# Gathering back the experts' rows: paced gathers, three pairs written back from ScalarE's loop, and slot numbers converted in an operation of their own

## The chip, the cores and the metric

The kernel runs on one core of a Trainium2 chip. The metric is the device time of one launch in microseconds. Three runs of the kernel before took 565.52, 563.89 and 565.66 us, with a median of 565.52 us. All times of the trace are counted from the start of the profiled execution's span.

## The reference, cut to what matters

The input x has 8 sequences of 256 tokens with 128 features. Four layers are applied, each as x + layer(layernorm(x)): a state-space block A with four heads, an expert block, a selective-scan block B (Mamba), and the same expert block again. The change concerns the expert block:

```python
logits = hidden @ router_w.T                  # 2048 tokens x 16 experts
top_vals, top_idx = top_k(logits, 1)          # one expert for each token
scores = sigmoid(top_vals)                    # at the chosen expert, 0 elsewhere
routed_in = hidden * score                    # only the chosen expert's row is not zero
gate, up = split(routed_in @ gate_up_proj[e])
expert_sum = (up * silu(gate)) @ down_proj[e]
shared = (silu(hidden @ Wg.T) * (hidden @ Wu.T)) @ Wd.T
return shared + expert_sum
```

## The kernel before, in words

Tokens lie on the 128 partitions in 16 blocks; four blocks are a group of 512 tokens (g = 0 to 3). Each engine has one program, written out in order, and the programs meet only at semaphores. A `Signal` is a semaphore whose value is known for each event; `wait_ge` on an engine blocks everything behind it on that engine.

**The expert block** runs twice, as turn t = 0 (after block A) and turn t = 1 (after the scan, to the end of the kernel). For each group, `choose` picks the expert of each token. `rank` on TensorE counts, and `place` on VectorE (line 977 on) turns the counts into the row of a DRAM tensor `by_expert` at which each token's features are kept, so that the tokens of one expert lie together. `place` multiplies the ranks by the one-hot choice and reduces by a maximum, written as an integer into `position` (line 983). GpSimd then sends the scaled rows with indirect DMAs (`send`, line 1794), one for each block of 128 tokens.

The rows come back as 31 slots of 128 rows, in 16 pairs: pair k holds slots 2k and 2k+1, and the last pair (k = 15) holds slot 30 alone. SyncE fetches 27 slots and ScalarE four (line 1563). For each pair TensorE computes gate and up (`expand`, line 732) and down (`contract`, line 744). ScalarE applies Silu (`gate_slots`, line 1552) and copies the product out of PSUM (`take_contracted`, line 1557), always two pairs behind. The results are then written back to `by_expert`: SyncE does it for pairs 0 to 13 (line 1943), in order, and ScalarE for pairs 14 and 15, which are `LAST_PAIRS`, in a loop of its own after the last copy (line 1577). Each of these DMAs moves one slot (64 KB) and is preceded by small register operations; the registers with the slots' addresses are loaded beforehand (line 1560 for ScalarE).

When all 31 slots are written back (`put_back`), GpSimd gathers the rows for the 16 blocks with indirect DMAs into `gathered` (line 1831). The gathers of group 2 wait for those of group 0 to land, and those of group 3 for those of group 1. VectorE adds a group to x when its four gathers have landed (`land`, line 1227; in turn 0 GpSimd does group 3, line 1870). Meanwhile TensorE works on the shared expert of groups 2 and 3 (line 680 for gate and up, line 693 for down, which VectorE adds to x at line 1167).

In turn 0 `enter_scan` follows: VectorE adds group 0 and takes its moments, ScalarE makes the root, VectorE scales, and TensorE turns the block (line 442) after its down product for group 2. In turn 1 each group of x goes to the output in one DMA of 256 KB from SyncE (line 1948) as soon as it is complete, and the kernel ends with the one of group 3.

**The scan** has 64 steps. In each step VectorE does two products (line 1290) and two scans (line 1296), GpSimd two products (line 1877) and ScalarE two exponentials (line 1685). Routing work of groups that are finished is put between the steps, among it `place` for groups 0, 1 and 2 of turn 1.

## Time and profile before

| | |
|---|---|
| median of three runs | 565.52 us |
| time of the profiled execution | 565.52 us |
| its span | 564.2 us |
| TensorE, VectorE busy | 467.7 us, 413.9 us |
| ScalarE, GpSimd busy | 317.0 us, 319.3 us |
| 32 indirect gathers (line 1831) | 31.5 us on GpSimd, 985 ns each |
| turn 0: first gather starts | 209.00 us |
| turn 1: first gather starts | 538.03 us |

The span is the time from the first to the last record of the execution; 1.3 us of the time lie outside it. A long row of busy shares says little here, because the stages have different limits: the stages have to be looked at one by one, with the chain of work that ended last.

### The profile page before, as it was taken

How to read it: one execution, taken by the hardware profiler on the slowest of the kernel's cores; microseconds unless marked ns; L12 is line 12 of the kernel's file. 1: busy time of each engine (PE TensorE's matmuls, PEld its weight loads, DVE VectorE, ACT ScalarE, POOL GpSimd, SP SyncE). 2: the span in 40 equal slices, each digit the busy share in tenths (PEclk: the TensorE clock that was granted, in tenths of full speed). 3: DMA queues.
4: the chain of work that ended last, by engine and by line, in shares of the span. 5: the costliest groups of instructions: out<-in, count | busy, mean ns of one | idle time of the engine just before them, and what ended most of it. 6: DMA issues, size and time to landing. Idle time of an engine off the chain costs nothing.

```text
span 564.2 us, 7407 instructions
## 1 busy us (share of the span) xinstructions
PE 467.7 (83%) x2102; PEld 267.8 (47%) x2102; DVE 413.9 (73%) x824; ACT 317.0 (56%) x656; POOL 319.3 (57%) x298
## 2 busy tenths in 40 slices
PE   0994878897979999989797998869776876799996
PEld 0742455565746985363232344223332331459973
DVE  4278969687256426399999799999999799564333
ACT  2574274655262644567674877787656952345611
POOL 1019743352544217246779778999799876442164
PEclk9997898998679999989998999999888989989999
DMA  8999930000004331155554455547544552014432
GB/s 292 424 327 333 322 132 1 1 2 20 19 29 120 111 113 52 51 159 138 157 150 133 130 157 149 138 130 185 153 133 127 166 150 56 20 48 118 125 82 89
DMA packets 39991, 73.94 MB, mean 131 GB/s; under 512 B 4368, under 2 KB 20240, under 8 KB 39184
## 3 DMA queue, kind: packets, MB, share of 16 engines
q1 hardware_dynamic: 35600, 67.00, 39.8%
q0 software_dynamic: 2048, 4.20, 2.5%
q10 hardware_dynamic: 2304, 2.29, 1.3%
q8 instruction: 17, 0.28, 0.2%
q14 instruction: 22, 0.18, 0.1%
HBM read 66.00 MB, written 26.28 MB: 164 GB/s over the span
## 4 chain that ended last, share of the span: by engine, by line
PE 35%; DVE 25%; issue 16%; ACT 13%; POOL 8%; DMA 2%; SPq 0%; DVEq 0%; POOLq 0%; ACTq 0%
DVE arena L1296 9%; PE psum L680 7%; PE psum L732 5%; POOL arena L1877 3%; PE psum L862 3%; DVE psum L1290 3%; ACT L1374 3%; POOL arena L1831 3%; PE psum L693 3%; PE psum L744 2%; ACT arena L1685 2%; PE psum L781 2%; ACT xn L1404 2%; PE psum L666 1%; PE psum L510 1%
## 5 line engine op out<-in xcount | busy, mean ns | idle before, releaser
L1877 POOL TENSOR_TENSOR arena<-arena 128x512 f32<-128x512 f32 x127 | 158.2, 1270 | 54.4 <-DVE arena L1296 54.1
L862 PE MATMUL psum<-arena,w 128*128 128x512 f32 x256 | 135.7, 645 | 28.2 <-POOL arena L1877 25.9
L1296 DVE TENSOR_TENSOR_SCAN arena<-arena,psum 128x512 f32<-128x512 f32 x128 | 148.4, 1200 | 7.7 <-ACT arena L1685 4.1
L1685 ACT ACTIVATE arena<-arena 128x510 f32<-128x510 f32 x128 | 87.2, 713 | 41.8 <-DVE arena L1296 39.4
L862 PEld LDWEIGHTS psum<-arena,w 128*128 128x128 f32 x256 | 45.4, 198 | 103.7 <-POOL arena L1877 79.5
L1290 DVE TENSOR_TENSOR psum<-psum,arena 128x512 f32<-128x512 f32 x128 | 81.5, 681 | 1.0 <-DMA arena<-bc_store 0.9
L680 PE MATMUL psum<-xnt,w 128*128 128x512 f32 x128 | 63.0, 643 | 0.0
L1762 POOL TENSOR_TENSOR arena<-arena 128x512 f32<-128x512 f32 x16 | 20.3, 1266 | 72.3 <-DVE arena L995 72.3
L1831 POOL DMA_INDIRECT arena<-by_expert,routes x32 | 31.5, 985 | 28.3 <-DMA by_expert<-arena 19.2
L1161 DVE TENSOR_TENSOR arena<-psum,arena 128x512 f32<-128x512 f32 x24 | 16.5, 690 | 34.0 <-PE psum L680 27.4
L1794 POOL DMA_INDIRECT by_expert<-xn,routes x32 | 32.3, 1008 | 13.7 <-issue 7.9
L680 PEld LDWEIGHTS psum<-xnt,w 128*128 128x128 f32 x128 | 25.5, 208 | 29.1 <-issue 28.6
L1374 ACT ACT_TABLE_LOAD x25 | 32.1, 1283 | 9.1 <-DMA c<-c_in 8.7
L732 PE MATMUL psum<-arena 128*128 128x128 f32 x248 | 33.1, 276 | 2.4 <-issue 2.4
L442 PE MATMUL psum<-w,xn 128*128 128x128 f32 x64 | 12.9, 347 | 26.4 <-DVE xn L945 13.2
L693 PEld LDWEIGHTS psum<-w,arena 128*128 128x128 f32 x256 | 30.5, 197 | 5.7 <-issue 5.7
L1527 ACT ACTIVATE arena<-psum 128x512 f32<-128x512 f32 x24 | 14.3, 596 | 33.4 <-PE psum L680 33.4
L1811 POOL COPY arena<-w 128x256 f32 x30 | 12.2, 414 | 36.1 <-PE psum L732 36.1
L1216 DVE TENSOR_TENSOR arena<-psum,arena 128x256 f32<-128x256 f32 (+1 forms) x32 | 13.3, 417 | 25.8 <-PE psum L744 18.4
L693 PE MATMUL psum<-w,arena 128*128 128x128 f32 x256 | 30.8, 280 | 1.8 <-DVE arena L1161 1.8
L732 PEld LDWEIGHTS psum<-arena 128*128 128x128 f32 x248 | 30.2, 192 | 2.8 <-issue 2.8
L781 PE MATMUL psum<-xnt,arena 128*128 128x512 f32 (+3 forms) x64 | 30.0, 600 | 0.0
(197 smaller groups left out, 815.5 us busy)
## 6 DMA issues: line engine op xcount, KB each, us to landing
arena<-bc_store SPq DMA_DIRECT2D x64, 512.0 KB, 4.9
by_expert<-w_in SPq DMA_DIRECT2D x4, 4096.0 KB, 43.3
w<-w_in SPq DMA_DIRECT2D x1, 4427.5 KB, 13.0
by_expert<-arena SPq DMA_DIRECT2D x56, 64.0 KB, 1.6
arena<-by_expert SPq DMA_DIRECT2D x54, 64.0 KB, 2.0
by_expert<-w_in SPq DMA_DIRECT2D x1, 1984.0 KB, 67.0
x<-x_in SPq DMA_DIRECT2D x4, 256.0 KB, 7.4
out<-x SPq DMA_DIRECT2D x4, 256.0 KB, 2.3
```

Source lines behind the costliest of these rows:

```text
L680: nc.tensor.matmul(b, weights[:, P * c:P * c + P], xnt_group(g), start=True, stop=True).then_inc(*made.inc((t, g, c)))
L693: r = nc.tensor.matmul(b[:, P * q:P * q + P], act_of(t, g)[:, c, P * q:P * q + P], wt("shared_down")[:, DM * c:DM * c + DM], start=(c == 0 ...
L732: r = nc.tensor.matmul(b[:, P * (2 * q + half):P * (2 * q + half) + P], chosen[s % len(chosen)][:, EF * half:EF * half + EF], xs_t[:, P * ...
L781: r = nc.tensor.matmul(by_sequence(b)[:, :, back:SEQ], taps[:, DC - 1 - back, P * c:P * c + P], by_sequence(xnt_group(g))[:, :, 0:SEQ - ba ...
L862: nc.tensor.matmul(bank(6 + c), ident, state[c][s % 3], start=False, stop=(n == DS - 1)).then_inc(*summed.inc((s, c)))
L1290: nc.vector.tensor_tensor(bank(2 + c), bank(c), bc_row[i][:, 0, :], ALU.mult).then_inc(*driven.inc((s, c)))
L1296: nc.vector.tensor_tensor_scan(state[c][s % 3], decay_b[c][s % 2], bank(2 + c), 0.0, ALU.mult, ALU.add).then_inc(*state_ready.inc((s, c)))
L1374: nc.scalar.preload_act_table_set(name)
L1685: nc.scalar.activation(live, seq, ACT.Exp, scale=a_neg[:, DS * c + n:DS * c + n + 1]).then_inc(*decay_ready.inc((s, c)))
L1794: nc.gpsimd.indirect_dma_start(by_expert, bass.IndirectOffsetOnAxis(position[:, j:j + 1], 0), xn[:, j, :], None).then_inc(*scatter[n // 2] ...
L1831: nc.gpsimd.indirect_dma_start(gathered[:, j, :], None, by_expert, bass.IndirectOffsetOnAxis(position[:, j:j + 1], 0)).then_inc(*read_back ...
L1877: nc.gpsimd.tensor_tensor(state[c][s % 3], state[c][s % 3], bc_row[s % len(bc_row)][:, 1, :], ALU.mult).then_inc(*y_done.inc((s, c)))
```

## The change

There are three edits. The first makes `place` write its maximum, now a sum, as a float, and adds a copy on VectorE which converts it to an integer in a tile of its own. The second makes the last three pairs ScalarE's (slots 26 to 30, five DMAs instead of three) and issues each pair's DMAs right after that pair's copy out of PSUM, inside the loop, instead of after the loop. The third changes the waits ahead of the gathers: in turn 0 each group from the second on waits until the group before it has landed, and in turn 1 group 2 waits for group 1 and there is no other wait.

```diff
-        routes = sb("routes", [P, NBLK * NE // 2 + 4 * NBLK])
+        routes = sb("routes", [P, NBLK * NE // 2 + 5 * NBLK])
...
-        LAST_PAIRS = range(n_pairs - 2, n_pairs)
+        LAST_PAIRS = range(n_pairs - 3, n_pairs)
...
-                nc.vector.tensor_reduce(position[:, js], by_token(own), AX.X, ALU.max).then_inc(*placed.inc((n, g)))
+                step(nc.vector.tensor_reduce(position[:, js], by_token(own), AX.X, ALU.add))
+                after_steps()
+                nc.vector.tensor_copy(position_int[:, js], position[:, js]).then_inc(*placed.inc((n, g)))
...
                     nc.scalar.activation(y_rows[:, s0:s0 + m, :], pair_bank[t, "down", k][:, 0:P * m].rearrange("p (q c) -> p q c", q=m),
                                          ACT.Copy).then_inc(*y_ready.inc((t, k)))
+                    if k in LAST_PAIRS:
+                        act.wait_ge(*y_ready[t, k])
+                        for s in pairs[k]:
+                            nc.scalar.dma_start(places[s], y_rows[:, s, :]).then_inc(*put_back[t].inc(s))
+
...
-                for k in LAST_PAIRS:
-                    act.wait_ge(*y_ready[t, k])
-                    for s in pairs[k]:
-                        nc.scalar.dma_start(places[s], y_rows[:, s, :]).then_inc(*put_back[t].inc(s))
                 for c in range(NSC):
                     shared(2, c)
...
                 for g in GROUPS:
-                    if g >= 2:
-                        pool.wait_ge(*read_back[g - 2][t, GB * (g - 1) - 1])
+                    if g == 2 or (g and t == 0):
+                        pool.wait_ge(*read_back[g - 1][t, GB * g - 1])
```

The indirect DMAs of lines 1794 and 1831 take their offsets from `position_int` instead of `position`.

## Rows read from the trace of the kernel before

**Rows 1.** The page: each engine's busy time, share of the span, instructions.
```profile
PE 467.7 (83%) x2102; PEld 267.8 (47%) x2102; DVE 413.9 (73%) x824; ACT 317.0 (56%) x656; POOL 319.3 (57%) x298
```
**Rows 2.** Chain that ended last, 555 us to the end: start, length, what.
```profile
557.39 3.78 DMA arena<-by_expert,routes
...
561.19 0.69 DVE x L1227
```
**Rows 3.** The same chain, 532 to 538 us.
```profile
536.15 1.61 DMA by_expert<-arena
```
**Rows 4.** Timeline of GpSimd, turn 1's gathers: start, length, engine, line, [idle before].
```profile
538.03 0.99 POOL L1831 DMA_INDIRECT arena<-by_expert,routes  x1 [9.82 <-DMA by_expert<-arena]
...
548.19 0.94 POOL L1831 DMA_INDIRECT arena<-by_expert,routes  x1 [0.30 <-issue]
...
555.69 1.39 POOL L1831 DMA_INDIRECT arena<-by_expert,routes  x1 [0.30 <-issue]
```
**Rows 5.** Line 1831, all 32 gathers: from issue to landing.
```profile
DMA to landing us min/median/max: 2.4/2.5/4.2
```
**Rows 6.** Timeline of VectorE at the end of turn 1.
```profile
555.58 1.28 DVE L1227 TENSOR_TENSOR x<-x,arena 128x512 f32<-128x512 f32 x2
559.65 0.69 DVE L1167 TENSOR_TENSOR x<-psum,x 128x512 f32<-128x512 f32 x1 [2.79 <-PE psum L693]
```
**Rows 7.** Line 1948, the outputs of groups 1 and 2, issued from 556.28 us.
```profile
DMA to landing us min/median/max: 2.3/2.9/3.5
```
**Rows 8.** Timeline of ScalarE, turn 1, the last three copies and the DMAs behind.
```profile
533.03 0.89 ACT L1557 ACTIVATE arena<-psum 128x256 f32<-128x256 f32 x2 [0.17 <-PE psum L744]
534.09 0.28 ACT L1557 ACTIVATE arena<-psum 128x128 f32<-128x128 f32 x1 [0.17 <-PE psum L744]
534.23 1.42 ACTq L1577 DMA_DIRECT2D by_expert<-arena  x3
535.75 0.60 ACT L1527 ACTIVATE arena<-psum 128x512 f32<-128x512 f32 x1 [1.38 <-PE psum L680]
```
**Rows 9.** Line 1577 in turn 1: ns least, median, most; time to landing.
```profile
L1577 ACTq DMA_DIRECT2D by_expert<-arena x3: 338/362/369, 534.2 to 535.3; - x3
...
DMA to landing us min/median/max: 1.7/1.8/1.9
```
**Rows 10.** Timeline of SyncE, 535.5 to 536 us: two of its DMAs back to back.
```profile
535.66 0.90 SPq L1943 DMA_DIRECT2D by_expert<-arena  x2
```
**Rows 11.** Timeline of VectorE: `place` in the scan, and two dependent small operations.
```profile
413.15 0.23 DVE L983 TENSOR_REDUCE routes<-psum 128x4 int32<-128x64 f32 x1
...
166.35 0.17 DVE L1186 TENSOR_REDUCE arena<-arena 128x1 f32<-128x16 f32 x1
166.56 0.15 DVE L1188 TENSOR_SCALAR arena<-arena 128x1 int32<-128x1 f32 x1
```
**Rows 12.** Timelines of GpSimd and VectorE in the scan, behind `place` of two groups.
```profile
419.19 2.50 POOL L1877 TENSOR_TENSOR arena<-arena 128x512 f32<-128x512 f32 x2 [0.23 <-DVE arena L1296]
...
375.04 2.33 DVE L1296 TENSOR_TENSOR_SCAN arena<-arena,psum 128x512 f32<-128x512 f32 x2 [1.36 <-issue]
```
**Rows 13.** Timeline of ScalarE at the start of turn 0's expert pairs.
```profile
175.01 0.60 ACT L1527 ACTIVATE arena<-psum 128x512 f32<-128x512 f32 x1 [1.12 <-PE psum L680]
177.55 1.88 ACTq L1563 DMA_DIRECT2D arena<-by_expert  x4
179.88 0.60 ACT L1542 ACTIVATE arena<-psum 128x512 f32<-128x512 f32 x1 [4.27 <-PE psum L717]
```
**Rows 14.** Timelines of ScalarE, GpSimd and VectorE, turn 0's write-back and gathers.
```profile
204.44 0.89 ACT L1557 ACTIVATE arena<-psum 128x256 f32<-128x256 f32 x2 [0.17 <-PE psum L744]
...
209.00 1.02 POOL L1831 DMA_INDIRECT arena<-by_expert,routes  x1 [9.38 <-DMA by_expert<-arena]
...
216.54 0.68 DVE L1227 TENSOR_TENSOR x<-x,arena 128x512 f32<-128x512 f32 x1
...
231.32 0.69 DVE L1161 TENSOR_TENSOR arena<-psum,arena 128x512 f32<-128x512 f32 x1 [3.38 <-PE psum L680]
```

More of the change, by code:

```diff
@@ L219, in build @@
         one_hot16 = routes[:, 0:NBLK * NE // 2].bitcast(BF16)
-        top, best, score, position = (routes[:, NBLK * NE // 2 + NBLK * i:NBLK * NE // 2 + NBLK * (i + 1)] for i in range(4))
-        position = position.bitcast(I32)
+        top, best, score, position, position_int = (routes[:, NBLK * NE // 2 + NBLK * i:NBLK * NE // 2 + NBLK * (i + 1)] for i in range(5))
+        position_int = position_int.bitcast(I32)
         piece = carve()
@@ L1793, in send @@
                 for j in js:
-                    nc.gpsimd.indirect_dma_start(by_expert, bass.IndirectOffsetOnAxis(position[:, j:j + 1], 0),
+                    nc.gpsimd.indirect_dma_start(by_expert, bass.IndirectOffsetOnAxis(position_int[:, j:j + 1], 0),
                                                  xn[:, j, :], None).then_inc(*scatter[n // 2].inc(j))
@@ L1827, in experts @@
                 for g in GROUPS:
-                    if g >= 2:
-                        pool.wait_ge(*read_back[g - 2][t, GB * (g - 1) - 1])
+                    if g == 2 or (g and t == 0):
+                        pool.wait_ge(*read_back[g - 1][t, GB * g - 1])
                     for j in blocks(g):
                         nc.gpsimd.indirect_dma_start(gathered[:, j, :], None, by_expert,
-                                                     bass.IndirectOffsetOnAxis(position[:, j:j + 1], 0)).then_inc(*read_back[g].inc((t, j)))
+                                                     bass.IndirectOffsetOnAxis(position_int[:, j:j + 1], 0)).then_inc(*read_back[g].inc((t, j)))
             for value, tile in ((1e-5, eps_ln), (1e-6, eps_rms), (float(np.pi / 2), quarter_turn), (1.0, one)):
```

## The prediction

> **What bounds the kernel now.** I read the page first: TensorE is busy for 467.7 us and VectorE for 413.9 us of 564.2 [rows 1]. No engine fills the span, so the stages must be taken singly, by the chain of work that ended last. At the end it runs through the gathers: the sixteenth starts at 557.39 us, lands 3.78 us later, at 561.17, and VectorE adds its group at 561.19 [rows 2]. Followed back, the gathers on GpSimd stand end to end from 538.03 us on, 1.25 us apart (0.94 busy, 0.30 issue) [rows 4], and the first one waits for a write-back of SyncE issued at 536.15 that takes 1.61 us, to 537.76 [rows 3]. So in turn 1 the write-back, the gathers and their landing are all on the path; a delay there is paid in full, less what the last landing gives back. In the scan VectorE's operations follow each other without idle time before them [rows 11], so a small operation added there is paid unless the engine idles later. In turn 0 the gathers feed VectorE's addition at 216.54 [rows 14] and have cover.
>
> **Part 1, the conversion.** `place` runs eight times. Each time a copy of 128x4 is added, and a wait between it and the reduction. The nearest pair is a reduction at 166.35 and the dependent small operation at 166.56: 0.21 us from start to start [rows 11]. I take 0.21 us each. The reduction itself stays at 0.23. Of the eight, the three of turn 0's groups 0 to 2 stand between other work of block A, and I cost them at nothing; the two of the groups 3 stand before the shared expert's products. If that cover were gone they would cost 5 x 0.21 = 1.05 us. In the scan there are three. Behind group 0's, VectorE idles for 1.36 us at 375.04, which ScalarE's work sets, so 0.21 is absorbed. Behind group 1's, at 413.15, GpSimd waits for VectorE at 419.19 [rows 11, 12] and passes the delay on; group 2's is like it. That is 2 x 0.21 = 0.42 us. Bounds: 0 if both are absorbed, 0.63 if all three pass.
>
> **Part 2, the write-back.** ScalarE loads two more addresses ahead of its fetches. Between its product's end at 175.61 and its first fetch at 177.55 it loads seven, 0.28 us each; two more make 0.55. Its fetches then end at 179.43 + 0.55 = 179.98, and with a gap of 0.10 (from the end of an issue at 535.65 to 535.75, [rows 8]) the first slots' copy starts at 180.08 instead of 179.88 [rows 13]: 0.20 us on TensorE's first pair. Between nothing and 0.55, I take 0.20, and nothing in turn 1.
>
> Now turn 1's last copies. Pair 13's copy starts at 533.03 and is over after half of 0.89, at 533.47. From a copy's start to the DMA behind it at 534.23 there are 0.14 for registers [rows 8]. Two DMAs of one pair are (1.42 - 0.37) / 2 = 0.53 apart and one takes 0.37 [rows 8, 9]. ScalarE waits for its own copy before it issues, so copy and issue no longer overlap, and the next copy stands behind the issues:
> pair 13: issues 533.61 and 534.14, free at 534.51; pair 14: copy 534.61 to 535.05, issues 535.19 and 535.72, free at 536.09; pair 15: copy 536.19 to 536.47, issue 536.61, landing 1.8 later [rows 9], at 538.41.
> SyncE loses two DMAs at 0.49 each (535.66 to 536.15, [rows 3, 10]) and its last lands at 537.76 - 0.98 = 536.78. So the last write moves from SyncE to ScalarE, and from 537.76 to 538.41: the gathers start 0.65 us later. The other end is 0.98 earlier, if SyncE still lands last. What ScalarE does next, the Silu at 535.75, comes some 1.3 us later, but its engine stood idle there and TensorE has a long down product before it needs that bank, so I cost it at nothing.
>
> **Part 3, the waits before the gathers.** In turn 1 group 2's first gather (548.19) now waits for the gather just before it, issued 1.25 us earlier, which lands after 2.5 us, the median [rows 4, 5]. With the 0.27 us from landing to start (537.76 to 538.03) this gather starts 2.77 us after its predecessor instead of 1.25: 1.52 us more. Queued behind it on GpSimd are seven gathers and nothing else; behind them VectorE's last addition and the output. The old waits cost nothing (0.30 us, as before every gather), and neither does dropping that of group 3. The last gather starts at 557.39 + 0.65 + 1.52 = 559.56.
> Its landing is the one place that gives back. It took 3.78 us beside two outputs of 256 KB issued from 556.28, which themselves took 2.3 and 3.5 us [rows 2, 7]. The new start is about when these end, so I take the median of 2.5 [rows 5] and get 562.06, 0.89 us later than 561.17. With 3.8 it would be 2.2 later.
> One gather, at 555.69, takes 1.39 instead of 0.94 us; it starts just after VectorE's addition at 555.58 [rows 4, 6]. I keep its 0.45. The Trainium skill (SBUF — State Buffer, on the port pair that VectorE and GpSimd share) says the pair is locked for a whole instruction when VectorE reads two SBUF inputs, and the second to come blocks. By that rule this row is a blocked gather, and since the additions of groups 1 and 2 will no longer be adjacent there may be two of them, 0.45 us more; if the starts miss each other it is 0.45 less.
> The skill's DMA: Bandwidth & Descriptors (the section on one GpSimd DMA) gives about 2.0 us fixed plus bytes over 436 GB/s, estimated 2.15 us for 64 KB. The trace has 2.5. By the page the stall would be 1.17 us and the sum 0.7 lower (stall and last landing).
>
> In turn 0 the same arithmetic on the copies from 204.44 on gives a last landing at 204.44 + 5.38 = 209.82 and the first gather at 210.09 instead of 209.00. The group's fourth starts 3.8 us later and lands at 216.4, against the addition at 216.54 [rows 14]: just hidden. Then each group waits. Group 1 starts at 216.7 and lands at 223.0, group 2 starts at 223.3 and lands at 229.6. VectorE idles for 3.38 us before 231.32 [rows 14]; the addition and moments of group 2 move into that gap. Group 3's addition waits on GpSimd, in the scan. Cost: nothing.
>
> **The sum.** 0.42 + 0.20 + 0.89 = 1.51 us on a profiled execution of 565.52 us (span 564.2 and 1.32 around it), which is also the median: 567.0 us. About 0.3% (1.7 us) is what a measurement of this kernel can tell from no change, and the sum lies just under it.
>
> **Rivals.**
> *SyncE still lands last.* ScalarE's issues are quick; the gathers start 0.98 earlier and the stall of 1.52 leaves the last at 557.93. For it: issue slots on ScalarE overlapped its copy at 534.23 [rows 8]. Against: the new wait is on the copy just made. Landing in 3.2, between the ends, at 561.1, the tail is even, and 0.62 remains: 566.1 us.
> *The gathers leave the end* (not slower). The stall is small and the last gather lands unhindered before VectorE's down addition ends at 560.34 [rows 6], so the last addition follows at 560.36 instead of 561.19: 0.83 us gained, 565.3 us, or 564.7 with the copies absorbed. It decides once the last gather lands before 560.34, so it must start by 557.8; my sum has it 1.7 us later.
> *The last landing stays at 3.8 us.* The outputs move later too, since group 2 lands later. 568.3 us.
> *Turn 0's waits show.* The place is VectorE's addition of group 0: its cover is only 0.14 us, and group 2's fills the 3.38 us almost wholly. If a gather there lands in 3.5 instead of 2.5 us, group 0 is about 1 us late, and everything up to the scan with it: 568.0 us or more.
> *The change does not do what it says* exists in a small form: in turn 0 it spaces gathers whose landing nobody awaits sooner. It is in the forecast.
>
> **How the numbers follow.** Forecast 0.55 (own range 566.0 to 568.0), SyncE last 0.13, gathers leave the end 0.10, landing stays long 0.12, turn 0 shows 0.10. The range from 564.8 to 568.9 reaches from the third case through the fourth; executions before spread down to 563.89. Slower by over 0.3% (above 567.2) holds some two fifths of the forecast and most of the last two cases: 0.43. Faster by over 0.3% needs the third case and the spread: 0.06. The rest, 0.51, is within 0.3%.
>
> **What would show it.** Part 1: a copy after each of the eight reductions, 0.2 us, and the end of the scan some 0.4 to 0.6 us later. Part 2: ScalarE's copies of pairs 14 and 15 about 1.1 us and 2.1 us later, its last issue near 536.6 (plus 0.6 from before), and the first gather released by ScalarE's DMA. Part 3: in turn 1 an idle time of 1.8 us on GpSimd before the ninth gather and no other, in turn 0 three such. Wrong would be a first gather earlier than 538.0, a last landing before 560.3, or an idle TensorE in 216 to 236 us.

## The result, and the profile after

The change makes the kernel slower. 15 runs of it have a median of 568.62 us (565.58 to 573.11), 15 runs of the kernel before, on the same chip, 565.52 us (562.94 to 567.87); the ratio is 1.0068 with a 95% interval of 1.0042 to 1.0095, so +3.8 us (+2.4 to +5.4). A ratio here is the one on record, worked out over all runs of both kernels, and not the quotient of the two medians: many runs of the kernel before lie close to 563 us or close to 567 us, and a median of a dozen jumps between the two. The forecast was 567.0 us, with "within 0.3%" as the likeliest outcome. Its sum was too small.

The profiled execution of the changed kernel spans 569.1 us against 564.2, 4.9 more. The page's first part, for [rows 1]:
```profile
PE 468.3 (82%) x2101; PEld 267.8 (47%) x2102; DVE 416.4 (73%) x832; ACT 316.7 (56%) x656; POOL 318.1 (56%) x298
```
VectorE has 8 instructions more and 2.5 us more of work. Eight copies at the forecast 0.21 us would be 1.7. Where the rest sits shows in the row of the copies' line; its columns are least, median and most ns, first and last start, shapes:
```profile
L985 DVE CAST routes<-routes x8: 169/183/1066, 116.6 to 498.2; 128x4 int32<-128x4 f32 x8
```
The median of 0.18 us is near what was forecast, and one copy takes 1.07 us. The timeline of VectorE finds it (start, length, engine, line, operation); the first three rows are group 1's `place` in the scan of turn 1, the rest is group 2's:
```profile
414.76 0.20 DVE L981 TENSOR_TENSOR psum<-psum,routes 128x64 f32<-128x64 f32 x1
415.00 0.23 DVE L983 TENSOR_REDUCE routes<-psum 128x4 f32<-128x64 f32 x1
415.26 0.24 DVE L985 CAST routes<-routes 128x4 int32<-128x4 f32 x1
...
474.96 0.20 DVE L981 TENSOR_TENSOR psum<-psum,routes 128x64 f32<-128x64 f32 x1
475.20 0.23 DVE L983 TENSOR_REDUCE routes<-psum 128x4 f32<-128x64 f32 x1
475.46 1.07 DVE L985 CAST routes<-routes 128x4 int32<-128x4 f32 x1
476.44 1.28 DVE L1292 TENSOR_TENSOR psum<-psum,arena 128x512 f32<-128x512 f32 x2
```
GpSimd's timeline at both places says why:
```profile
412.98 4.95 POOL L1880 TENSOR_TENSOR arena<-arena 128x512 f32<-128x512 f32 x4
...
474.01 2.49 POOL L1880 TENSOR_TENSOR arena<-arena 128x512 f32<-128x512 f32 x2 [0.93 <-DVE arena L1298]
476.58 0.23 POOL L1781 TENSOR_SCALAR routes<-routes 128x4 f32<-128x4 f32 x1
```
Two products of about 1.25 us start at 474.01 and 475.23. The copy starts 0.23 us into the second and is over with it, at 476.5. Group 1's copy starts at 415.26, just before the second of its four products ends (at 415.48), and is over at 415.51. A copy that meets a product lasts until the product ends; it is short or long by where in the product it starts.

To see what this does to the end, I compared the start of the same VectorE instruction in both traces, counted from the start of the span. The shift grows by 1.10 us at this copy (from 2.13 to 3.23), and is 4.71 at the additions near 541 us. The part before the scan (+1.8) is not the change's: such shifts lay between -2.2 and +3.9 in the other profiled executions, of both signs. Inside the scan 0.35 us is added ahead of this copy, 0.28 of it at group 1's; group 0's 0.28 is there at 357 us and gone by 380, as was forecast. Behind the copy another 1.5 us is added, between the router's last products and the expert pairs. This is TensorE there, before and after:
```profile
494.28 10.34 PE L680 MATMUL psum<-xnt,w 128*128 128x512 f32 x20
...
508.02 0.60 PE L717 MATMUL psum<-w,arena 128*128 128x128 f32 x4
```
```profile
497.45 9.12 PE L680 MATMUL psum<-xnt,w 128*128 128x512 f32 x20
...
511.08 0.63 PE L717 MATMUL psum<-w,arena 128*128 128x128 f32 x4 [0.93 <-DMA arena<-by_expert]
```
The twenty products of the shared expert take 1.2 us less after, and the first product of an expert now waits 0.93 us for its fetched rows. From the first of them to the expert it is 13.7 us before and 13.6 after: next to nothing gained. The cause of the 1.2 us is TensorE's clock. These are the rows of a table of stretches (stretch, its length, busy us of PE, PEld, DVE, ACT and POOL, the granted clock as a share of 2.4 GHz, DMA share, GB/s), again before and after:
```profile
490.00:500.00 10.00, 8.32 (x42) 4.72 (x41) 6.00 (x22) 6.81 (x13) 4.66 (x5) 0.83 0.05 16
...
510.00:520.00 10.00, 10.00 (x92) 10.00 (x91) 4.31 (x12) 6.47 (x15) 2.40 (x6) 1.00 0.40 110
```
```profile
490.00:500.00 10.00, 8.32 (x45) 4.60 (x44) 5.97 (x29) 7.42 (x17) 2.81 (x4) 1.00 0.05 15
...
510.00:520.00 10.00, 7.98 (x56) 7.66 (x55) 2.85 (x7) 3.72 (x8) 1.20 (x3) 0.83 0.45 128
```
Each kernel has one stretch of 3.4 us at 1.2 GHz here (0.83 over 10 us). Before, it lies at 494 us in the shared products. The fourth fetch lands there 0.7 us before TensorE comes to it, so of the 1.2 us that the stretch costs about half is hidden under the fetch. After, it lies at 513 us among the expert pairs, where TensorE is busy for all of the 3.4 us: there it is paid, and from the first expert to 541 us the kernel takes 1.66 us longer than before. Ahead of each stretch TensorE had stood idle: before, for 0.78 and 0.90 us behind the router's steps between 490.9 and 494.1 us; after, for the 0.93 us behind the fetch and another 1.09 us up to 512.79.

The end of turn 1, for [rows 2 to 4]: the timeline of GpSimd (first, last of group 1, first of group 2), and the chain's last pieces (start, length, what).
```profile
542.94 0.99 POOL L1834 DMA_INDIRECT arena<-by_expert,routes  x1 [10.01 <-DMA by_expert<-arena]
...
551.76 0.95 POOL L1834 DMA_INDIRECT arena<-by_expert,routes  x1 [0.30 <-issue]
554.53 0.95 POOL L1834 DMA_INDIRECT arena<-by_expert,routes  x1 [1.83 <-DMA arena<-by_expert,routes]
```
```profile
541.13 1.55 DMA by_expert<-arena
542.68 0.26 issue
...
563.35 2.76 DMA arena<-by_expert,routes
566.11 0.02 issue
566.13 0.69 DVE x L1229
```
Against a shift of 4.72, the first gather is 0.19 us late (542.94 - 4.72 - 538.03), the ninth idles for 1.83 us, the last lands after 2.76 us and not 3.78, and the last addition is 0.22 late. ScalarE's side, for [rows 8, 9]:
```profile
537.75 0.38 ACT L1559 ACTIVATE arena<-psum 128x256 f32<-128x256 f32 x1 [0.17 <-PE psum L744]
538.30 0.90 ACTq L1564 DMA_DIRECT2D by_expert<-arena  x2
539.25 0.39 ACT L1559 ACTIVATE arena<-psum 128x256 f32<-128x256 f32 x1 [1.11 <-PE psum L744]
539.80 0.84 ACTq L1564 DMA_DIRECT2D by_expert<-arena  x2
540.69 0.28 ACT L1559 ACTIVATE arena<-psum 128x128 f32<-128x128 f32 x1 [1.05 <-issue]
541.13 0.34 ACTq L1564 DMA_DIRECT2D by_expert<-arena  x1
```

### The profile page after: what moved, and what is told of

It is laid out like the page before. It is cut to its first block, busy times and chain, and to the rows that moved or that the text cites. A ratio compares the mean times of both kernels' runs of the same rounds, so it can differ in the third digit from the quotient of the medians.

```text
span 569.1 us, 7422 instructions
## 1 busy us (share of the span) xinstructions
PE 468.3 (82%) x2101; PEld 267.8 (47%) x2102; DVE 416.4 (73%) x832; ACT 316.7 (56%) x656; POOL 318.1 (56%) x298
## 4 chain that ended last, share of the span: by engine, by line
PE 32%; DVE 26%; issue 17%; ACT 11%; POOL 9%; DMA 4%; SPq 1%; ACTq 0%; DVEq 0%; POOLq 0%
DVE arena L1298 10%; PE psum L732 5%; PE psum L680 5%; POOL arena L1880 4%; DVE psum L1292 3%; PE psum L862 3%; PE psum L744 2%; POOL arena L1834 2%; PE psum L693 2%; PE psum L781 2%; ACT L1376 2%; ACT xn L1406 2%; ACT arena L1688 1%; POOL by_expert L1797 1%; PE psum L717 1%
## 5 line engine op out<-in xcount | busy, mean ns | idle before, releaser
L1292 DVE TENSOR_TENSOR psum<-psum,arena 128x512 f32<-128x512 f32 x128 | 81.4, 681 | 0.7 <-DMA arena<-bc_store 0.7
L732 PE MATMUL psum<-arena 128*128 128x128 f32 x248 | 34.4, 283 | 2.6 <-issue 2.6
L442 PE MATMUL psum<-w,xn 128*128 128x128 f32 x64 | 12.8, 346 | 25.8 <-DVE xn L945 13.2
L732 PEld LDWEIGHTS psum<-arena 128*128 128x128 f32 x248 | 31.5, 199 | 3.0 <-issue 3.0
```

The source lines that it names most:

```text
L732: r = nc.tensor.matmul(b[:, P * (2 * q + half):P * (2 * q + half) + P], chosen[s % len(chosen)][:, EF * half:EF * half + EF], xs_t[:, P * ...
L1292: nc.vector.tensor_tensor(bank(2 + c), bank(c), bc_row[i][:, 0, :], ALU.mult).then_inc(*driven.inc((s, c)))
```

## The experiments

Ratios are to the kernel before, run in turn with it on the same chip (such a set of kernels is called a series here), with 95% intervals; each has some 12 runs of its own and 23 to 35 of the kernel before, unless said otherwise. "Group 2" is group 2 of turn 1 throughout.

### The three parts singly

**Part 1 alone**, the conversion in `place`, all eight:
```diff
-                nc.vector.tensor_reduce(position[:, js], by_token(own), AX.X, ALU.max).then_inc(*placed.inc((n, g)))
+                step(nc.vector.tensor_reduce(position[:, js], by_token(own), AX.X, ALU.add))
+                after_steps()
+                nc.vector.tensor_copy(position_int[:, js], position[:, js]).then_inc(*placed.inc((n, g)))
```


> The kernel before with part 1 alone (float positions and a copy to integers). Theory A, read from the two traces: the added copy waits for GpSimd's long products on the shared SBUF ports (1.07 us instead of 0.17 to 0.24 behind group 2 of turn 1), and what it delays ends in the addresses of SyncE's fetches; so this part is most of the change, +1.5 to +3 us. Theory B, the prediction's sizes: +0.4 us, not to be told from nothing.

Measured: 570.34 us (6 runs), ratio 1.0122 (1.0076 to 1.0167). The same kernel a second time:

> Part 1 alone once more, since its first six timed runs gave a wide interval (+0.8 to +1.7%). Theory A (1.4 us in the scan and 1.5 to 2 us behind it): +3 us, near +0.55%, so the first timing was high by chance. If it repeats at +6 us, part 1 costs more alone than in the full change and theory A lacks something.

Measured: 571.14 us, 1.0095 (1.0057 to 1.0132). Part 1 is the bulk of the change's cost. In both profiles of this kernel, and in no other, a second copy met GpSimd: group 2's in turn 0 took 1.06 us, where it took 0.17 elsewhere. Whether this makes part 1 alone dearer was not tested.
```profile
152.36 1.06 DVE L985 CAST routes<-routes 128x4 int32<-128x4 f32 x1
```
```profile
152.36 1.04 POOL L1786 TENSOR_TENSOR xn<-xn,routes 128x512 f32<-128x512 f32 x1 [0.56 <-ACT routes L1425]
```

**Part 2 alone**, three pairs written back by ScalarE, each behind its copy (`LAST_PAIRS` from `n_pairs - 3`, the DMAs moved into `take_contracted`).

> The kernel before with part 2 alone (three last pairs on ScalarE, issued inside the loop). Theory A: turn 1's gathers start 0.2 us later as measured from the last copies, and two more address loads cost 0.2 us: +0.2 to +0.6 us. Theory B: +0.85 us (0.65 and 0.20).

Measured: 567.71 us, 1.0021 (0.9986 to 1.0056). Its profile has the first gather 0.18 us late and the last addition 0.20 us early, both against the shift at the additions near 541 us.

**Part 3 alone**, the gathers' waits:
```diff
-                    if g >= 2:
-                        pool.wait_ge(*read_back[g - 2][t, GB * (g - 1) - 1])
+                    if g == 2 or (g and t == 0):
+                        pool.wait_ge(*read_back[g - 1][t, GB * g - 1])
```


> The kernel before with part 3 alone (the new waits ahead of the gathers). Both theories: group 2 of turn 1 starts 1.5 us later; the last landing falls from 3.8 to 2.5 to 2.8 us because the outputs of groups 1 and 2 are through; net +0.1 to +0.6 us. In turn 0 three idle times of 1.8 us on GpSimd that cost nothing. If the waits were the cause of the miss: +1.5 us or more.

Measured: 565.80 us, 1.0003 (0.9967 to 1.0039). The stall is there, on GpSimd, and the last addition comes only 0.23 us late:
```profile
551.21 0.95 POOL L1831 DMA_INDIRECT arena<-by_expert,routes  x1 [2.60 <-DMA arena<-by_expert,routes]
```

**Parts 2 and 3 without part 1.**

> The changed kernel with part 1 taken back (parts 2 and 3 alone). Theory A: +0.3 to +1 us over the kernel before, so some 3 us less than the changed kernel. Theory B: +1.1 us. A third theory, that any moved instruction shifts the phases of clock and fetch whatever the edit, would have e1, e2, e3 and this one all near +3 us or scattered without regard to their parts.

Measured: 566.74 us, 1.0036 (1.0005 to 1.0066); in the profile the last addition is 0.24 us late. This one pair of profiles accounts for 0.2 of the measured 2.0 us, and the interval begins at 0.3 us. The gathers in all profiles, further below, give 0.7.

### Which of the eight copies

**The copy from PSUM**: as part 1, but the sum goes to four free columns of the rank bank and the copy reads them.
```diff
-                step(nc.vector.tensor_reduce(position[:, js], by_token(own), AX.X, ALU.add))
+                step(nc.vector.tensor_reduce(rank_bank[n, g][:, 4 * NE * GB:4 * NE * GB + GB], by_token(own), AX.X, ALU.add))
                 after_steps()
-                nc.vector.tensor_copy(position_int[:, js], position[:, js]).then_inc(*placed.inc((n, g)))
+                nc.vector.tensor_copy(position_int[:, js], rank_bank[n, g][:, 4 * NE * GB:4 * NE * GB + GB]).then_inc(*placed.inc((n, g)))
```


> Part 1 alone, but the sum is reduced into free columns of the rank's PSUM bank and the copy to integers reads it there. Theory A (the copy blocks on SBUF ports that GpSimd holds): no copy of 1.07 us behind group 2 of turn 1, all eight at about 0.2 us, and the time 1 to 3 us below the kernel with part 1 alone. Theory C (the copy is slow there for another reason, or any eight extra operations cost this): as slow as part 1 alone.

Measured: 570.11 us, 1.0063 (1.0035 to 1.0091). The copies no longer meet anything, least, median and most ns:
```profile
L985 DVE CAST routes<-psum x8: 161/161/163, 117.8 to 498.7; 128x4 int32<-128x4 f32 x8
```
and yet it costs about as much as the whole change in its first measurement. Against part 1 alone (1.0122 and 1.0095, in other series) it is 1.8 to 3.3 us cheaper, which is the theory's 1 to 3 us, but what stays is not small. It is taken up again below.

**Only the scan's three copies, and all but these** (`if n == 3 and g < NGRP - 1`, and its opposite, choose the conversion; elsewhere the reduction writes the integer as before).

> Part 1 only for groups 0 to 2 of turn 1, whose place stands in the scan; the other five write integers directly. Theory A: all of part 1's cost is here, +3 us, of it 1.4 in the scan (0.3 behind group 1 and 1.1 behind group 2) and the rest behind it. Prediction's sizes: +0.4 us.

> Part 1 only for the four groups of turn 0 and group 3 of turn 1. Theory A and the prediction: no change, within 0.3 us. Rival: the copies ahead of the slots' addresses in group 3 are what delays SyncE's fetches, then +1 us or more and TensorE waits for a fetch at its first turned slots of turn 1.

Measured: 1.0037 (1.0005 to 1.0069) and 1.0034 (1.0001 to 1.0066). Both halves read alike, and their intervals are wide: this split alone tells nothing apart. The second half holds the five copies that were forecast at nothing, and its interval begins just above nothing.

**A delay in the place of the copy**: the kernel before, with the multiplication of `place` made five times for group 2.
```diff
-                step(nc.vector.tensor_tensor(own, ranks, one_hot16[:, NE * GB * g:NE * GB * (g + 1)], ALU.mult))
+                for _ in range(5 if (n, g) == (3, 2) else 1):
+                    step(nc.vector.tensor_tensor(own, ranks, one_hot16[:, NE * GB * g:NE * GB * (g + 1)], ALU.mult))
+                    after_steps()
```


> The kernel before, with the multiplication of place repeated four more times for group 2 of turn 1 alone (it gives the same values), which adds about 1.0 us to VectorE there and nothing else; integers are written directly. Theory A2: what costs is a delay of VectorE at this place whatever makes it: 1.0 us in the scan, and about 2 us more behind it, since TensorE's half-clock stretch near 494 us moves to near 509 us, where it is not hidden; +3 us. Rival: a delay there costs just its own length, +1.0 us.

Measured: 568.90 us, 1.0037 (1.0006 to 1.0067). The profile: VectorE 1.07 us later at this place, the half-clock stretch at 511 us instead of 494, another 1.7 us behind it. No copy is in this kernel; the time at this place is what costs.

**Group 2's copy alone, the other seven alone, the full change without that one copy, and the full change**, in one series. The first chooses the conversion by `if (n, g) == (3, 2)`, the second and third by `if (n, g) != (3, 2)`.

> The conversion at one place only, turn 1's group 2 (the copy that took 1.07 us in the kernel with all eight). Theory A (this one copy is the bulk of part 1: it waits for GpSimd's product, and the 1.1 us late groups behind it cost about twice that again): a copy of about 1.07 us, VectorE's addition near 541 us some 2.5 to 3 us later than before, +0.5% in time, that is most of the +0.7% to +1.2% of the kernels with all eight. Rival B (every added copy counts alike, wherever it stands): an eighth of it, +0.1%. Rival C (the copy and its 1.07 us are hidden, and part 1's cost comes from elsewhere, for instance the sum in place of the maximum or other places): within 0.2% of before although the copy takes 1.07 us.

> Seven of the eight conversions, all but turn 1's group 2, whose reduction writes the integer as before. Theory A: no copy over 0.3 us, and +0.1 to +0.3% only. Rival B (all count alike): seven eighths of part 1's cost, +0.6 to +1.0%. Rival C: as B, since the cost would be elsewhere.

> The full change, but turn 1's group 2 writes its integer without a copy. Theory A: +0.2 to +0.4%, what parts 2 and 3 had without the conversion (+0.36%), and group 2 no later than group 1. Rivals B and C: as the full change, +0.6 to +0.7%.

> The full change again, in the same call as its three neighbours, as their yardstick. All theories: +0.68% (0.4 to 0.95). If it reads +1.0% or more, part 1 alone, which read +1.2% and +0.95% in other calls, is no dearer than the whole; if it reads 0.7% or less beside a smaller number for the kernel without group 2's copy, that difference is the one copy's price within one call.

Measured:
```
only group 2's copy          568.74 us   1.0074 (1.0041 to 1.0106)
the other seven              566.19 us   1.0008 (0.9974 to 1.0042)
full change but group 2      567.16 us   1.0049 (1.0017 to 1.0081)
full change (5 runs)         570.97 us   1.0122 (1.0082 to 1.0163)
```
One copy of 128x4 costs 0.74% by itself, and the seven others cost nothing that this series can tell (up to 0.42%). Taken out of the full change it gives back 0.73% (1.0122 to 1.0049). That is the theory's picture, and the rival by which each copy counts alike falls: its seven eighths should have read +0.6% or more. The full change, with only 5 runs, read 1.0122 here and 1.0068 in its first series, with intervals that overlap only from 1.0082 to 1.0095; part 1 alone, at 1.0122 and 1.0095, is thus not shown to be dearer than the whole.

**The same single copy from PSUM against from SBUF**, in one series; the first has the reduction and copy of the PSUM kernel above, for group 2 only.

> The one conversion of turn 1's group 2, with the sum reduced into four free columns of its PSUM bank, so that the copy reads PSUM and writes SBUF. Theory A1 (the price is the 1.07 us in which the SBUF-to-SBUF copy stands beside GpSimd's product): a copy of about 0.16 us, group 2 some 0.2 us later instead of 1.1, and within +0.2% of before. Theory A2 (what costs is that one more dependent operation stands at this place at all, and 0.2 us is as dear as 1.1, because what follows turns on it): +0.5% or more in spite of the quick copy, as the kernel with all eight copies from PSUM read +0.63%.

> The conversion of turn 1's group 2 alone with its copy from SBUF, again, as the yardstick of its neighbour in the same call. Both theories: a copy of 1.07 us and +0.5 to +0.9% (it read +0.74%).

Measured: 565.25 us, 0.9998 (0.9960 to 1.0035), and 568.65 us, 1.0043 (1.0010 to 1.0077). VectorE in the two, from PSUM first:
```profile
473.13 0.23 DVE L984 TENSOR_REDUCE psum<-psum 128x4 f32<-128x64 f32 x1
473.39 0.16 DVE L986 CAST routes<-psum 128x4 int32<-128x4 f32 x1
473.48 1.30 DVE L1295 TENSOR_TENSOR psum<-psum,arena 128x512 f32<-128x512 f32 x2
```
```profile
476.93 0.22 DVE L984 TENSOR_REDUCE routes<-psum 128x4 f32<-128x64 f32 x1
477.19 1.06 DVE L986 CAST routes<-routes 128x4 int32<-128x4 f32 x1
478.17 1.28 DVE L1295 TENSOR_TENSOR psum<-psum,arena 128x512 f32<-128x512 f32 x2
```
The same two operations at the same place, with GpSimd's products beside them in both. Only where the sum is kept, and so the source of the copy, differs, and with it 0.9 us of the copy's length; the cost goes from +0.4% (+0.7% in the other series) to nothing. The two intervals still overlap; the granted clock of each run, taken up next, parts them. The price is the wait, not one more dependent operation. What stays of the PSUM kernel with all eight copies is open: its +0.63% lies beside +0.08% for the seven from SBUF and -0.02% for group 2's from PSUM, whose intervals together reach up to +0.77%.

**The granted clock of each run.** Each run's time is on record with the mean granted clock of its execution. Over the 150 runs of the kernel before in these series, a run with 0.01 more of it is 3.7 us shorter (correlation -0.84), so most of the spread between runs is the clock's. Taking this slope out of both kernels of a comparison leaves the differences of their means, in us, with intervals of about 95%:
```
group 2's copy alone, twice          +3.3 (2.3 to 4.2)    +2.7 (2.2 to 3.2)
group 2's copy from PSUM             -0.1 (-0.7 to 0.4)
delay without copy                   +3.2 (2.5 to 4.0)
part 1, twice                        +4.0 (3.0 to 4.9)    +3.2 (2.4 to 4.1)
scan's three copies                  +2.6 (1.5 to 3.8)
all but the scan's three             +2.0 (1.1 to 2.9)
the other seven                      +1.2 (0.2 to 2.2)
all copies from PSUM                 +3.7 (2.7 to 4.7)
part 2                               -0.3 (-1.2 to 0.6)
part 3                               -0.1 (-1.0 to 0.8)
parts 2 and 3                        -0.1 (-0.8 to 0.7)
full change but group 2              +0.9 (-0.3 to 2.1)
full change (5 runs)                 +4.9 (3.8 to 6.1)
later loads (next section)           -0.4 (-1.2 to 0.5)
part 1, later loads                  +1.8 (0.9 to 2.6)
full change, later loads             +1.3 (0.4 to 2.2)
```
This leaves out whatever a change does to the mean clock itself. It holds the main reading with narrower intervals: about 3 us for the delay at group 2's place, whatever makes it, and nothing for the same copy from PSUM. It also says that the other copies are not free, between 1.2 and 3.7 us in three kernels. Which of them costs this was not tested; one candidate is group 3's, since the first fetch of turn 1 is issued 8.77 us behind the start of its `place` in the ten profiles with this copy and 8.52 us in the ten without, on average.

### The wait for the fetch behind it

The first product of an expert waited for its fetched rows in the changed kernel and, for 1.4 us, in part 1 alone. SyncE loads one more address behind each of its first fetches, which in the kernel before stand 0.85 us apart. I moved these loads to behind the fifth fetch and those that follow it, in the kernel before, with part 1, and with the full change:
```diff
-                    if n + KNOWN < len(fetched):
-                        find(fetched[n + KNOWN])
+                    if n >= GB and n - GB + KNOWN < len(fetched):
+                        find(fetched[n - GB + KNOWN])
```


> The kernel before, with SyncE's seven late address loads moved behind its fifth to eleventh fetch instead of its first to seventh, so that the first four fetches of each turn (the slots that TensorE turns first) are issued 0.47 us apart instead of 0.85. Theory F (TensorE's first turned slots of turn 1 are set by these fetches as soon as TensorE runs at its full clock ahead of them): fetches ready about 1.1 us earlier; the kernel gains up to 1 us where TensorE had full clock there and nothing where not: -0.5 us. Rival (the fetches have 1.5 us to spare, as the prediction assumed): nothing.

> Part 1 alone with the same move of the address loads. Theory F: in turn 1 TensorE's wait of 1.4 us for a fetch ahead of its first turned slots falls to 0.3 us or less, and the time is about 1.1 us below part 1 alone. Rival (the wait is only where TensorE spends what the clock gives it elsewhere): the wait is gone but the time is the same.

> The changed kernel with the same move. Theory F: 1 us below the changed kernel, +2.5 us over the kernel before. Rival: the same as the changed kernel, +3.8 us.

Measured: 563.61 us, 0.9986 (0.9947 to 1.0025); 568.77 us, 1.0054 (1.0020 to 1.0087); 568.49 us, 1.0054 (1.0017 to 1.0091). The wait is gone or down to 0.2 us in the profiles, and both kernels with the conversion stay 0.7% above the one without; the copy's 1.07 us stand in both. But the fair neighbour of part 1 with the later loads is part 1 alone, in the same series, and against it the move gains 1.6 us in the mean (3.5 gained to 0.3 lost), 1.5 with the clock taken out, where the theory said 1.1. In the two profiles with the conversion the first expert starts 12.5 and 12.6 us behind group 3's `place`, and in all others 13.2 to 14.0. And the wait goes with the place of the half-clock stretch: the eight profiles with a stretch between 509 and 515 us are those with a wait of 0.9 to 1.6 us for the fetch ahead of it, while of the twelve others eleven wait 0.2 us or less and one 0.84. So the wait is not shown to be without a price; a part of what follows the copy may well run through it. None of the three kernels is shown to beat the kernel before.

### All profiles side by side

Three shifts of VectorE against the kernel before (just ahead of group 2's `place`, just behind it, at the additions near 541 us), and TensorE's half-clock stretches from 470 to 520 us (start + length):
```
                              ahead  behind  541 us   stretches
full change                   +2.13  +3.23   +4.71    513+3.4
part 1                        -1.27  -0.17   +1.60    509+3.4
scan's three copies           -1.83  -0.73   +6.15    478+10.2, 512+6.8
delay without copy            +0.24  +1.31   +3.02    511+3.4
part 1, again                 +0.39  +1.50   +2.44    480+3.4, 497+3.4
part 1, later loads           +0.73  +1.83   +4.51    481+10.2
full change, later loads      +2.07  +3.17   +2.60    none
group 2's copy alone          -1.74  -0.63   +1.05    509+3.4
full change, again            +2.52  +3.63   +7.06    482+10.2
group 2's copy alone, again   +3.86  +4.96   +6.24    515+3.4

before                         0      0       0       494+3.4
part 2                        +2.84  +2.85   +3.27    497+3.4
part 3                        +1.32  +1.32   +1.52    495+3.4
parts 2 and 3                 -2.13  -2.14   -2.12    491+3.4
all but the scan's three      +1.88  +1.88   +1.72    495+3.4
later loads                   +1.78  +1.78   +1.98    496+3.4
full change but group 2       +0.57  +0.57   +0.72    494+3.4
group 2's copy from PSUM      +0.06  +0.26   +0.31    494+3.4
all copies from PSUM          +3.54  +3.76   +5.80    514+3.4
the other seven copies        +2.09  +2.10   +3.87    513+3.4
```
Above, the ten kernels in which the place takes 1.1 us more: behind it they lose a median of 1.7 us more (mean 2.1). Below, the ten others: a median of 0.2 (mean 0.5). The difference in mean is 1.7 us, and with the 1.1 us at the place it makes 2.8 us, 0.49% of the time. That is the size of the +0.74%, +0.43% and +0.37% measured for group 2's copy alone, twice, and for the delay. The mean leans on one profile, the scan's three copies with 6.9 us; by the medians it is 1.5 us. What is lost goes with the stretch more than with the copy: the two below that have it at 513 and 514 us lose 1.8 and 2.0 us, the eight others between -0.2 and +0.4.

**The gathers in all profiles.** Up to here the end of the kernel was read from one profile of the kernel before, and that one is not typical. Measured from the same addition near 541 us, the first gather starts 4.16 us ahead of it on average in the fourteen profiles without part 2 (2.8 to 4.6; 3.67 in the kernel before) and 3.47 in the six with it (3.43 to 3.49): 0.69 us later. The last addition starts 19.05 us behind it on average in the fourteen without part 3 and 19.71 in the six with it (19.6 to 19.9): 0.67 us later. In seven of those fourteen it starts at 18.7 us, right behind VectorE's addition of the down product, as in the kernel with group 2's copy alone:
```profile
560.70 0.69 DVE L1172 TENSOR_TENSOR x<-psum,x 128x512 f32<-128x512 f32 x1 [2.79 <-PE psum L693]
561.50 0.69 DVE L1232 TENSOR_TENSOR x<-x,arena 128x512 f32<-128x512 f32 x1
```
There the gathers had already left the end of the kernel, and parts 2 and 3 bring them back to it. Counted at the last addition instead of at 541 us, the ten profiles with the delay are 1.5 us (0.8 by the medians) later behind the place than the ten others, so 2.6 us with the 1.1.

## Why the prediction was wrong, point by point

**The step that failed** is the term of part 1: "The nearest pair is a reduction at 166.35 and the dependent small operation at 166.56: 0.21 us from start to start. I take 0.21 us each", and of it the copy of group 2, "group 2's is like it". That copy took 1.07 us, and put 1.10 where 0.21 stood. The nearest pair was the wrong one to take: at 166 us no GpSimd product ran beside it. And the prediction quoted the lock that decides this, for gathers only. The Trainium skill (SBUF — State Buffer, SBUF: two separate sides) says that a GpSimd operation and a VectorE operation in a two-port mode exclude each other for a whole instruction, and its "DVE blocks DMA" box counts an fp32 copy from SBUF to SBUF among these; the Trainium skill also (VectorE: DVE Perf Modes, Why PSUM operands drop a tier) says that a PSUM operand cannot use that mode. The runs agree: 1.07 us from SBUF, 0.16 from PSUM. The copy starts 0.23 us behind the product, it is the copy that waits, and it is over 0.03 us behind the product's end. What the trace adds is that the copy is let in between two products: behind group 1's the next product starts at once and keeps its 1.28 us. The kernel before had the rows to apply it. This is GpSimd beside group 2's `place` there:
```profile
471.88 2.50 POOL L1877 TENSOR_TENSOR arena<-arena 128x512 f32<-128x512 f32 x2 [0.92 <-DVE arena L1296]
```
with the second product from 473.10 to 474.38. `place`'s reduction starts at 473.07 there, a copy behind it at about 473.33, and a copy that waits for the product is over at 474.38: 1.05 us.

**What a delay there is worth** failed too. The forecast passed it on one to one ("GpSimd waits for VectorE at 419.19 and passes the delay on"). Measured, the 1.1 us are followed by about 1.5 to 1.7 us more on average. The account that the profiles suggest is that the late routing moves where TensorE is slow: before, its 3.4 us at 1.2 GHz fell into shared products where half of their cost was hidden under the fetch; with the delay of 1.1 us they mostly fell among the expert pairs, or a stretch of 10.2 us appeared near 480 us. Term forecast 0.42, measured about 2.6 to 3.3 us (+0.49% by the profiles at 541 us, 2.6 us at the last addition, +0.59% as the mean of the two measurements of the single copy). That the stretch is elsewhere than before is seen in 8 of the 10 profiles with the delay; why it falls where it does was not tested. Two of the ten others have it at 513 and 514 without the delay, so a single execution can't be read for it.

**The other seven copies**: two were as said, group 0's absorbed and group 1's passed on (0.28 us against 0.21; it took 0.24 us by the luck of starting at a product's end). The five forecast at nothing are not shown to be free: the seven read +0.08% (-0.26 to +0.42), the five alone +0.34% (0.01 to 0.66), and 1.2 and 2.0 us with the clock taken out. That term was put at nothing for cover that was named and not measured; what it is stays open.

**Part 2, the address loads in turn 0**: forecast 0.20 for the first slots' copy on ScalarE, and that copy comes 5.08 us behind the product ahead of it instead of 4.87, so 0.21 late. Whether it is passed on can't be told: the profiles shift there by -2.2 to +3.9 us. **The write-back in turn 1**: forecast 0.65 late, measured 0.19 in this pair of profiles and 0.69 over all twenty. The forecast of 0.65 lands on the average partly by luck, since it was worked out from the one profile and two of its sizes were off for that. That the last write moves to ScalarE and that copies and issues no longer overlap was right: less the shift, the copies of pairs 14 and 15 are 0.99 and 1.88 us late, 1.1 and 2.1 were forecast. The gaps behind the issues, the copies and the second pair's issues are each 0.02 to 0.06 us shorter than I had taken them, so the last issue is at 541.13 - 4.72 = 536.41 and not 536.61; and it lands after 1.55 us, not 1.8 ([rows 9] had three DMAs close together, here the last stands alone). 0.20 + 0.25 is the difference of 0.65 and 0.19, to 0.01.

**Part 3**: forecast a stall of 1.52 on top of the usual 0.30; measured 1.83 in all, so 1.53. The last landing fell from 3.78 to 2.76 where 2.5 was forecast, the rival with 3.8 did not come, and the blocked gather of [rows 4], which I had kept, took 1.01 us and not 1.39. With 0.38 for this and 0.1 in the spacing of the others, 0.19 + 1.53 - 1.02 - 0.38 - 0.10 = 0.22 us for the tail, against 0.89 forecast; part 3 alone and parts 2 and 3 show 0.23 and 0.24. All four are against the same profile of the kernel before, with its late gathers. Over all profiles the tail costs 0.67 us, near the forecast, although the forecast took the gathers to be on the path always and in seven of the fourteen profiles without part 3 they are not. The stall isn't fixed either: in part 3 alone it was 2.60 us, behind gathers that had started 0.7 us earlier, and the last gather started 16.9 us behind the addition near 541 us in all six.

**Turn 0**: forecast no cost, and it has none: group 0's addition starts at 218.28 us, which is 216.54 and the shift of 1.74. There are three stalls as said, the idle times in brackets:
```profile
218.12 0.95 POOL L1834 DMA_INDIRECT arena<-by_expert,routes  x1 [1.95 <-DMA arena<-by_expert,routes]
...
224.70 0.95 POOL L1834 DMA_INDIRECT arena<-by_expert,routes  x1 [1.86 <-DMA arena<-by_expert,routes]
...
231.22 1.28 POOL L1834 DMA_INDIRECT arena<-by_expert,routes  x1 [1.79 <-DMA arena<-by_expert,routes]
```
Group 2's addition and moments fill the gap of [rows 14], almost wholly, and TensorE has no idle time that it had not before (0.87 us at 217.64, as at 215.90):
```profile
230.98 0.69 DVE L1229 TENSOR_TENSOR x<-x,arena 128x512 f32<-128x512 f32 x1 [3.85 <-DMA arena<-by_expert,routes]
...
233.06 0.69 DVE L1163 TENSOR_TENSOR arena<-psum,arena 128x512 f32<-128x512 f32 x1
```
The shift stays at 1.7 us on both sides of it (1.74 at 231, 1.73 at 250).

**None of the four rivals** was what happened: they all lay in the gathers, and the cost was in the part that I had taken for the surest. That the measured 568.62 us lies inside the range of 564.8 to 568.9 is luck: the range was widened for gathers, and the 3 us came from a copy.

**The account.** Group 2's copy is the difference of 0.73% within one series, and 2.6 to 2.8 us by the profiles. The tail adds 0.7 us. With 3.8 us measured (2.4 to 5.4) that leaves 0.3 to 0.5 us, inside the interval. Parts 2 and 3 with the other copies read +0.49% (0.17 to 0.81), 2.8 us, of which the tail explains 0.7; the rest may be the other copies, and whether it is real stays open.

## What to carry to other kernels

Before a small copy or scalar operation from SBUF to SBUF is priced on VectorE by its like, lay GpSimd's timeline beside every place where it is added: where a product runs there, the copy is over when the product is, so its price is what is left of that product, not its median. If it has to stand there, let its source be PSUM. And a delay in a serial stage can cost more than itself; two profiles of one kernel show how much of a shift belongs to nobody. The same holds for the path: what ended last in one profile of the kernel before, the gathers, ended last in at most half of the profiles with the same code there.

## What the runs showed of the hardware

A copy of 128x4 took 0.17 us alone and 0.16 us from PSUM. From SBUF, started 0.23 us behind a GpSimd product of 1.27 us, group 2's took 1.06 to 1.07 us in all nine profiles that have it; started 0.01 us behind one of 1.04 us, it took 1.06. In all of them it was over 0.03 us behind the product's end. VectorE's product of two inputs, one of them in PSUM, kept its length beside the same GpSimd products (L1292: 1.28 us for two).

TensorE's half-clock stretches come in lengths of 3.4, 6.8 and 10.2 us in these traces. Code that is the same up to that point has them at other places: near 240 and 302 us the kernel before has 3.4 us each time, the kernel with part 3 alone 6.8. These are the rows at both places, before and with part 3:
```profile
236.00:246.00 10.00, 7.30 (x33) 5.33 (x32) 8.33 (x23) 9.58 (x18) 0.00 (x0) 0.83 0.66 187
298.00:308.00 10.00, 6.08 (x10) 2.57 (x11) 9.89 (x12) 5.62 (x9) 9.92 (x9) 0.83 0.41 106
```
```profile
236.00:246.00 10.00, 7.30 (x29) 5.44 (x28) 8.44 (x23) 9.58 (x18) 0.00 (x0) 0.67 0.81 185
298.00:308.00 10.00, 6.03 (x9) 2.35 (x8) 9.90 (x13) 5.62 (x9) 9.92 (x8) 0.66 0.39 109
```
Between 231 and 320 us this kernel's shift goes from -0.11 to +1.26. The runs of the kernel before spread from 561.4 to 569.3 us over all series; that spread is why 12 runs a side still leave intervals of 0.7%.
